# Three passes over the tokens instead of one block at a time, and MLP items put in bins with at most two adapters

## What is computed

```python
# layer 0: one full 512x512 matrix per item (8 of them), then kernel + gated LoRA of rank 32 per group of 8 items
h0 = einsum('bsi,boi->bso', x, L0_cond_weight[itok_B_3_7])
x  = x + (h0 @ kernel + bias + LoRA_group(h0) + LoRA_shared(h0))
# layer 1: gated MLP, 1376 wide, with LoRA of rank 16 per item (16 adapters) on gate, up and down
gate = x @ W_gate.T + 0.5 * (x @ A_gate[i].T) @ B_gate[i].T      # i = itok_B_2_6, one per item
up   = x @ W_up.T   + 0.5 * (x @ A_up[i].T)   @ B_up[i].T
act  = silu(gate) * up
h    = act @ W_down.T + 0.5 * (act @ A_down[i].T) @ B_down[i].T
# then a linear layer with a LoRA whose rank (8, 16, 32, 64) is chosen per token by a softmax over h
x  = x + (h @ W.T + b + routed_LoRA(h))
```

## Time and profile before

| | us |
|---|---|
| median of 3 runs | 758.69 (756.89 to 759.4) |
| the profiled execution | 757.57 |
| its span, first to last instruction | 755.7 |
| TensorE busy | 732.2 |
| VectorE, ScalarE, GpSimd busy | 280.6, 289.0, 368.9 |

### The profile page before, as it was taken

The page is one execution under the profiler, slowest core; times in us unless marked ns, Lnnn a source line. Parts: engine busy times, 40 slices in busy tenths (PEclk is TensorE's granted clock), DMA queues, the critical chain, the costliest instruction groups (busy, mean ns, idle before and its releaser), DMA issues.

```text
span 755.7 us, 11627 instructions
## 1 busy us (share of the span) xinstructions
PE 732.2 (97%) x3814; PEld 617.5 (82%) x3814; DVE 280.6 (37%) x521; ACT 289.0 (38%) x507; POOL 368.9 (49%) x310
## 2 busy tenths in 40 slices
PE   4799989999999999999999999999999999999997
PEld 2677878888888888888888888888888888888885
DVE  2787674311112763211114753111117642111134
ACT  1774653434232435342334235323314344333221
POOL 0234562786764204877645017876642038866400
PEclk9999999999999999999999999999999999999999
DMA  8864561344426041343333313443350413433201
GB/s 316 346 236 175 224 236 45 116 134 125 114 78 215 5 153 62 115 134 114 103 130 125 111 42 104 135 125 101 96 198 24 154 42 114 138 112 97 76 1 56
DMA packets 31228, 95.00 MB, mean 126 GB/s; under 512 B 4544, under 2 KB 4672, under 8 KB 29152
## 3 DMA queue, kind: packets, MB, share of 16 engines
q1 hardware_dynamic: 22656, 65.28, 25.9%
q0 software_dynamic: 8544, 29.37, 12.4%
HBM read 84.67 MB, written 9.96 MB: 125 GB/s over the span
## 4 chain that ended last, share of the span: by engine, by line
PE 93%; DVE 2%; DMA 2%; ACT 1%; issue 1%; SPq 0%; ACTq 0%; DVEq 0%
PE psD L1042 11%; PE psD L1043 11%; PE psD L1044 10%; PE psG L1042 7%; PE psG L1044 7%; PE psG L1043 7%; PE psU L1042 7%; PE psU L1043 7%; PE psU L1044 7%; PE psD L1100 2%; PE psD L1101 2%; PE psD L1102 2%; DMA x_all<-in_x_t 2%; PE psT L1044 1%; PE psT L1043 1%; PE psT L1042 1%
## 5 line engine op out<-in xcount | busy, mean ns | idle before, releaser
L461 POOL TENSOR_TENSOR gu_lo<-gu_raw,gu_hi 128x1024 fp32r<-128x1024 f32 x44 | 107.1, 2433 | 90.5 <-ACT gu_hi L574 87.0
L486 POOL DMA_INDIRECT ab<-in_ab,idx_row x88 | 87.3, 992 | 48.7 <-POOL idx_row L480 33.0
L952 DVE TENSOR_TENSOR act_f<-psU,silu 128x512 f32<-128x512 f32 x44 | 30.4, 692 | 192.1 <-PE psU L1044 184.8
L461 POOL TENSOR_TENSOR bu_lo<-ab,bu_hi 128x512 fp32r<-128x512 f32 x44 | 56.9, 1293 | 84.5 <-ACT bu_hi L574 84.5
L708 ACT ACTIVATE silu<-psG 128x512 f32<-128x512 f32 x44 | 26.3, 597 | 151.3 <-PE psG L1044 151.1
L461 POOL TENSOR_TENSOR dn_lo<-dn_raw,dn_hi 128x512 fp32r<-128x512 f32 x44 | 56.9, 1292 | 39.3 <-ACT dn_hi L574 39.3
L1042 PE MATMUL psG<-x_hi,gu_hi 128*128 128x512 f32 x176 | 72.8, 414 | 0.0
L1044 PE MATMUL psG<-x_hi,gu_lo 128*128 128x512 f32 x176 | 69.2, 393 | 0.0
L1042 PE MATMUL psD<-act_hi,dn_hi 128*128 128x512 f32 x176 | 69.0, 392 | 0.0
L1043 PE MATMUL psD<-act_lo,dn_hi 128*128 128x512 f32 x176 | 69.0, 392 | 0.0
L1042 PE MATMUL psU<-x_hi,gu_hi 128*128 128x512 f32 x176 | 68.9, 391 | 0.0
(11 more groups left out here) (256 smaller groups left out, 1797.1 us busy)
## 6 DMA issues: line engine op xcount, KB each, us to landing
gu_raw<-in_gu SPq DMA_DIRECT2D x44, 512.0 KB, 3.5
dn_raw<-in_dn SPq DMA_DIRECT2D x44, 256.0 KB, 2.6
cond_w_raw<-in_cond_w SPq DMA_DIRECT2D x8, 1024.0 KB, 5.8
x_all<-in_x_t SPq DMA_DIRECT2D x4, 1024.0 KB, 10.2
tok<-h_scratch SPq DMA_DIRECT2D x4, 1024.0 KB, 7.4
x_t<-in_x_t SPq DMA_DIRECT2D x4, 1024.0 KB, 5.1
out_t<-out_b SPq DMA_DIRECT2D x16, 256.0 KB, 3.8
ab<-in_ab,idx_row POOLq DMA_INDIRECT x88, 3.1
```

Of the source, the lines that this page charges most:

```text
L461: pool.tensor_tensor(dst, x, hi, ALU.subtract).then_inc(s, 1)
L486: pool.indirect_dma_start(ab[:, par, g, :], None, a["ab"], bass.IndirectOffsetOnAxis(idx_row[:, par, g:g + 1], 0)).then_inc(S[f"ab_in{par} ...
L952: dve.tensor_tensor(act_f[:], psU[:], silu[:], ALU.mult).then_inc(S["act_f_s"], 1)
```

## The change

The block loop is taken apart into three passes over the four blocks of 512 tokens: first layer for all, MLP for all, second layer for all. x and its sums stay in `x_all` the whole time, and the MLP's result goes to `h_all`; the second load of x and the sum of x1_hi and x1_lo go away.

For the MLP pass the items are put in 16 bins of four, so that a bin holds items of at most two adapters: adapter a's bin holds its own items and, where it has fewer than four, those that other adapters have over. The places are worked out on VectorE (`fill_bins` in the opening, `find_fillers`, `rank_items`, `place_fillers` and `place_items` in condition blocks 13 to 16) and turned into addresses by two small matmuls. The MLP's input is gathered item by item from `x_all` (`high_x1`, `low_x1`: 16 copies each per block) and its output put back item by item (`put_h`: 16 copies on ScalarE for half of the features, 16 on VectorE for the other half).

Eight items now need 4 x 16 = 64 rows for their LoRA factors. The tile of 128 rows holds them twice: hi above, lo below (for `bu` and `ad`, split by VectorE's `low_bu` and the lower half of `ad`), and `stacked` multiplies this with hi and lo of the other side in two matmuls instead of three. A_gate and A_up stand in the two halves of one tile, so that `ranks` runs once, and `turn_a` transposes two tiles instead of four. In the diff, `...` marks what is left out.

```diff
+            def stacked(ps, w, xh, xl, start, stop):
+
+                pe.matmul(ps, w, xh, start=start, stop=False, skip_group_check=True)
+                return pe.matmul(ps, w, xl, start=False, stop=stop, skip_group_check=True)
...
+            def high_x1(t):
+                act.wait_ge(S["x1_f"], C * NTB)
+                act.wait_ge(S["up_ps"], NF * t)
+                for q in range(TB // BT):
+                    at = bin_cols(act, t * (TB // BT) + q)
+                    for j in range(BI):
+                        i = (q * BI + j) * ITEM_T
+                        high(x1_hi[:, :, i:i + ITEM_T], x_all[:, :, bass.ds(at[j], ITEM_T)], S["x1_hi_s"])
...
+            def put_h(t):
+                act.wait_ge(S["h_ps"], C * t + 2)
+                for q in range(TB // BT):
+                    at = bin_cols(act, t * (TB // BT) + q)
+                    for j in range(BI):
+                        i = (q * BI + j) * ITEM_T
+                        act.activation(h_all[:, 0:2, bass.ds(at[j], ITEM_T)], psD[:, 0:2, i:i + ITEM_T], ACT.Copy
+                                       ).then_inc(S["h_out0"], 1)
...
                 chunks(act, step, 1, 1)
 
+                if t < NTB - 1:
+                    high_x1(t + 1)
+                    high_at(t + 1)
+                    high_gu(0, NF * t + NF, NF * t + NF)
                 act.wait_ge(S["td_m"], t + 1)
-                high(td_hi[:], tm[:], S["td_hi_s"])
...
+                high(td_hi[:], tm[:, 1, :], S["td_hi_s"])
+                if t < NTB - 1:
+                    high_bu(0, (NF // 2 + 1) * (t + 1) + 1)
+                    high_tg(t + 1, 0)
+                    high_tg(t + 1, 1)
+                put_h(t)
...
+                if t < NTB - 1:
+                    low_x1(t + 1)
                 dve.wait_ge(S["td_ps"], NF * (t + 1))
                 dve.wait_ge(S["tg_lo_s"], 2 * (t + 1))
-                masked(psT[:], S["td_m"])
+                masked(tm[:, 1, :], psT[:], slice(0, P), t, S["td_m"])
+                if t < NTB - 1:
+                    low_at(t + 1)
                 dve.wait_ge(S["td_hi_s"], t + 1)
...
+                low(td_lo[:], tm[:, 1, :], td_hi[:], S["td_lo_s"])
+                if t < NTB - 1:
+                    dve.wait_ge(S["td_lo_s"], t + 1)
+                    open_tg(t + 1)
+                    low_bu(0, NF * t + NF)
+                put_h(t)
...
+            def ranks(t):
+
+                pe.wait_ge(S["t0_m"], NTB)
+                pe.wait_ge(S["ad_lo_s"], NF * t)
+                pe.wait_ge(S["at_lo_s"], NGT * (t + 1))
+                for g in range(NGT):
+                    cols = slice(g * GT, g * GT + GT)
+                    pe.wait_ge(S["x1_lo_s"], TB // ITEM_T * t + GI * (g + 1))
+                    for c in range(C):
+                        mm = product(psX[:, cols], both(at_hi, at_lo, al, g, slice(c * P, c * P + P)),
+                                     both(x1_hi, x1_lo, al, c, cols), g == 0 and c == 0, c == C - 1)
+                mm.then_inc(S["tg_ps"], 1)
...
                         for g in range(NGT):
                             cols = slice(g * GT, g * GT + GT)
-                            mm = product(ps[:, cols], both(bu_hi, bu_lo, al, par, g, slice(k * P, k * P + P)),
-                                         both(tg_hi, tg_lo, al, k, cols), False, True)
+                            mm = stacked(ps[:, cols], bu[:, par, g, k * P:k * P + P], tg_hi[:, k, cols],
+                                         tg_lo[:, k, cols], False, True)
                         mm.then_inc(S[s], 1)
...
                 chunks(pe, step, 2, 1)
+                if t < NTB - 1:
+                    turn_a(t + 1)
                 down((NF - 1) % 2, NF * (t + 1), False, True)
+                if t < NTB - 1:
+                    ranks(t + 1)
```

More of the change, by code:

```diff
@@ L898, in _, with low_h0 @@
-            dve.wait_ge(S["wf_lo_s"], 2)
-            def body(t, more):
-                def low_at(k):
-                    dve.wait_ge(S["at_hi_s"], 4 * t + k + 1)
-                    low(at_lo[:, k % 2, :], A_BANK[k][:], at_hi[:, k % 2, :], S["at_lo_s"])
+            def low_h0(t):
+                hi, lo = HT0[t % 2]
+                for c in range(C):
+                    dve.wait_ge(S["h0t_hi"], C * t + c + 1)
+                    low(lo[:, c, :], H0_BANK[c][:], hi[:, c, :], S["h0t_lo"])
@@ new lines, in first_layer, with low_at, low_x1 @@
+                add(3)
+            for t in range(NTB):
+                first_layer(t)
+            def low_at(t):
+                for g in range(NGT):
+                    dve.wait_ge(S["at_hi_s"], NGT * t + g + 1)
+                    low(at_lo[:, g, :], A_BANK[g][:], at_hi[:, g, :], S["at_lo_s"])
+            def low_x1(t):
+                for q in range(TB // BT):
+                    at = bin_cols(dve, t * (TB // BT) + q)
+                    for j in range(BI):
+                        i = (q * BI + j) * ITEM_T
+                        dve.wait_ge(S["x1_hi_s"], TB // ITEM_T * t + q * BI + j + 1)
+                        low(x1_lo[:, :, i:i + ITEM_T], x_all[:, :, bass.ds(at[j], ITEM_T)],
+                            x1_hi[:, :, i:i + ITEM_T], S["x1_lo_s"])
@@ L945, in step, with low_bu, body @@
+            dve.wait_ge(S["item1_ready"], 1)
+            dve.wait_ge(S["x1_f"], C * NTB)
+            low_at(0)
+            low_x1(0)
+            dve.wait_ge(S["mask1_ready"], 1)
+            open_tg(0)
+            def low_bu(par, n):
+                dve.wait_ge(S["bu_hi_s"], n + 1)
+                low(bu[HALF:P, par], ab[HALF:P, par, :, P:STAB], bu[HALF:P, par], S["bu_lo_s"])
+            low_bu(0, 0)
+            def body(t):
                 def step(fc, j, par):
                     n = NF * t + fc
+                    first = isinstance(fc, int) and fc == 0
+                    if not last(fc):
+                        low_bu(1 - par, n + 1)
@@ L1195, in body @@
-                ranks(0)
-                turn_a(2)
-                turn_a(3)
+                kern(0)
+                kern(1)
+                pe.wait_ge(S["be_l"], t + 1)
+                pe.wait_ge(S["t0_lo"], t + 1)
+                lora(0)
+                lora(1)
+                if t < NTB - 1:
+                    turn_h0(t + 1)
+                kern(2)
+                lora(2)
+                kern(3)
+                lora(3)
+            for t in range(NTB):
+                first_layer(t)
@@ L1199, in down, with body @@
+            turn_a(0)
+            ranks(0)
+            def body(t):
                 def down(par, n, opens, closes):
@@ L1205, in down @@
                         cols = slice(g * GT, g * GT + GT)
-                        mm = product(psT[:, cols], both(ad_hi, ad_lo, al, par, slice(g * P, g * P + P)),
-                                     both(act_hi, act_lo, al, par, cols), opens and g == 0, closes)
+                        mm = stacked(psT[:, cols], ad[:, par, g * P:g * P + P], act_hi[:, par, cols],
+                                     act_lo[:, par, cols], opens and g == 0, closes)
                     mm.then_inc(S["td_ps"], 1)
```

888 lines of the change are left out of this document (528 added, 360 removed).

## The result

The changed kernel took 782.27 us, median of 4 runs (781.16 to 782.84), against 758.82 for the kernel before on the same chip: ratio 1.030 [1.028, 1.033]. The forecast was 769 with a range of 748 to 780, so the sign is right and the size is not: the loss is 23.5 us, not 10.

What follows compares the result with a forecast made beforehand. TensorE, busy 97% of 755.7 us, was taken as the bound. Less 46.7 of work, plus 37.5 for three boundaries, 8.9 entry and 11.5 exit gives 766.9 span; with 1.9 around it, 769 us, range 748 to 780.

Steps and rivals of the forecast that it cites:

- What bounds it: Kernel before: TensorE fills each block end to end; only fewer columns gain time, only holes in its queue lose it.
- What the change takes away: TensorE's work: 31.7 us from 44 chunks, 11.5 from `ranks`, 3.5 from `turn_a`, together 46.7 us less.
- the exit: From MLP pass to second layer: TensorE waits 9.7 us for put_h and h_hi/h_lo, plus 1.75 for clock: 11.5 us.
- the entry: From first layer into MLP pass: TensorE waits for gathered items, 8.9 us lost; chunk 1 then waits at most 0.3.
- one boundary: Between two blocks of the MLP pass: two holes, each with 1.75 us of clock loss, 12.5 us; three make 37.5.
- Hole A: At each boundary between MLP blocks, TensorE waits before `ranks` for the gather and at_lo: 4.6 us.
- Hole B: At each boundary between MLP blocks, TensorE waits before chunk 1 for put_h, gu_hi, then gu_lo: 4.4 us.
- None comes near 9.87 us: Inside an MLP chunk, VectorE's and GpSimd's changed work stays well below the 9.87 us chunk, so nothing becomes late.
- The clock: After each boundary hole and the exit's, TensorE runs at 1.2 GHz for about 4 us, costing 1.75 us each.
- Rival 3: VectorE and GpSimd slow each other; nine elementwise steps per boundary take half as long again, 3.3 us each time: 779; chance 0.10.
- Rival 1: Clock stays at 2.4 GHz over the holes, 13 us less: 756; chance 0.22 including mixtures.
- Rival 2: Register loads run ahead of the engines, so a group of copies costs 0.8 us: 732, faster; chance 0.10.

Runs made afterwards that it cites:

- second run with fillers: Changed kernel plus dummy 128-column fp32 products, 22 before `ranks` and 18 before chunk 1 at the three boundaries: 778.0 us.
- last kernel: Changed kernel with all register loads placed earlier, ScalarE's entry gather before gu_hi and bu_hi, bu_lo behind act_lo, wf_lo in four parts: 731.3 us, 0.964 of the kernel before.

## Why the prediction was right and wrong

*What bounds it* held: TensorE's columns, and holes in its queue. *What the change takes away* held: chunks 9.88 apart against 9.87, and in the changed kernel TensorE's busy time less what the windows show as lost to the clock, 704.9 - 19.0, is 685.9 against the 685.5 of the forecast. No hole over 0.5 us opened in the first pass; the exit's was 10.0 (forecast 9.7), the entry's 7.2 (5.6 + 1.2).

The direction and the kinds of loss were right; the step that failed is the sum of one boundary, 12.5 us, with what each engine's queue still has to do before TensorE is let go. The loss was short by 14.0 us of span (780.9 against 766.9), 9.0 of idle time and 5.0 of half clock. By terms:

- *Hole A*, 17.8 against 3 x 4.6. The step "ends at 2.8 + 3 x 2.04 + 0.9" is the one that was short: the first group started 3.4 us after the last up product, the groups were up to 2.4 apart, and at the first boundary the fourth took 3.04, since gu_lo had just started (0.96 in the run with gu_lo cut short). It was 4.0 us short.
- *Hole B*, 14.5 against 3 x 4.4. The size was near in part by luck, since another queue ended the hole. I had ScalarE's put_h, then gu_hi, then gu_lo at 30.5 as the last; ScalarE's groups came 1.64 apart instead of 1.8, and what came last was VectorE: its put_h, bu_lo at 2.07 and ad_lo. "VectorE's own put_h, low_bu and ad_lo end at about the same time, so that they add nothing" is the sentence that failed, for it priced bu_lo at 0.68. It was 1.3 us short.
- *Entry and inside the pass*: 1.65 us before chunks 1 and 2 of the first block, where I had at most 0.3, and 1.7 at t = 2 behind wf_lo, which I had not costed at all because it had been covered before. "None comes near 9.87 us" is true of busy time and missed the order: in a pass whose engines enter late, an operation of 7.41 us shows. With 0.4 more at the entry itself and 0.3 at the exit this closes the 9.0.
- *The clock*: the half rate came after every hole, as forecast, but lasted longer. Chunk 1 of the first boundary ran at 1.2 GHz from 328.0 to 332.8, which costs 2.4, and `ranks` about 2.2, against 1.75 each. I had taken the one stretch of 4 us in the earlier trace rows as its length. And the second run with fillers shows that such a term is not simply added: removing 11.5 us of it at the boundaries gave back 4.3.

*Rival 3* is what happened on top of the forecast, and it was priced at half again for every step, by kern_lo in the earlier trace rows. As measured it is a wait for the other's instruction: nothing for the steps with an input in PSUM, and a factor of 3.5 for a short one with two inputs in SBUF. The trace of before had a row that showed more than kern_lo did, which I had not read. x_sum and x_lo both have two inputs in SBUF and 512 columns, yet their means are 1300 and 693 ns. Ten of the 16 x_sum take 0.68 us; the other six, which stand beside GpSimd's ae_lo and gu_lo, take 1.78 or 2.88. No x_lo meets an elementwise operation of GpSimd. (Count, busy us, mean ns; the second line gives the least, median and most of x_sum.)

```profile
L968 DVE TENSOR_TENSOR x_sum<-x_hi,x_lo 128x512 f32<-128x512 f32 x16 | 19.8, 1300 | 0.0
...
L968 DVE TENSOR_TENSOR x_sum<-x_hi,x_lo x16: 678/684/2885, 250.1 to 737.6; 128x512 f32<-128x512 f32 x16
...
L746 DVE TENSOR_TENSOR x_lo<-x_t,x_hi 128x512 fp32r<-128x512 f32 x16 | 11.1, 693 | 11.2 <-ACT x_hi L574 11.2
```

*Rival 1* (clock held) is refuted for the changed kernel by its windows (0.85, 0.84, 0.83). *Rival 2* (loads hidden, 732) did not come by itself, as I argued from the earlier trace rows: a queue of instructions waiting on a hole has no backlog. It did come for single groups that had one: at the entry VectorE's second group started 0.23 us after a first that took 2.33, instead of the usual 1.14. Its price of 732 was near: without any loads the kernel takes 738.7. That 731.3 was reached with the loads placed by hand under other work is partly luck, since that kernel has bu_lo and wf_lo moved too.

What stays open: why two groups of the gather are once 2.4 us apart instead of 2.0 (it is not ScalarE's x_hi: the copies for the group that starts at 300.94 were over at 299.80); what the 3.3 us of busy time in the last kernel are; and how much of the remaining 16.4 us of idle could be covered.

## What to carry to other kernels

When a stage that covered latencies is taken out, list every instruction that stood under it and write down, for each engine's queue, what is last before TensorE is let go; a price of "0, it was covered" must be worked out again at each new hole. Addresses read from registers cost their engine's time where they stand, so load them in a stretch where that engine is idle anyway: here this alone turned 3% slower into 1% faster, and with the rest into 4%. A loss by the clock is not to be added to a loss by waiting before it is known that no other engine is late at the same place. An elementwise step that costs little alone should be priced by what GpSimd runs beside it, whenever both its inputs lie in SBUF.

## What the runs showed of the hardware that I had not expected

- VectorE (with both inputs in SBUF) and GpSimd did not run at once but one after the other: 64 x 512 with both inputs in SBUF took 0.69 us alone and 2.45 in the median beside gu_lo, 3.79 at most; 128 x 2048 took 7.41 instead of 2.29, having stood through three GpSimd instructions in a row; a GpSimd copy of 0.18 took 2.26.
- Register loads stand 0.28 us apart in VectorE's queue; four of them left it idle for 1.39 us, sixteen in a row for 5.6; four of them and four copies of 64 columns are 2.01 us on VectorE and 1.64 on ScalarE. Once they are loaded ahead, sixteen x_lo copies run in 3.31 us.
- The clock fell to 1.2 GHz after holes shorter than those forecast here: in the second run with fillers `ranks` came 2.54 us after them, the granted clock was 0.5 from 307.9 to 311.3 and its products 0.21 us apart, then 0.12; the stretch of the earlier trace rows, after 2.3 us of idle time, says the same.
- A 128 x 128 product in plain fp32 is two records and 0.227 us (9.09 / 40), where a transpose of the same size is one of 0.11.
